# Adaptive-norm mixture-of-experts kernel: weights laid out by the host, condition matrices gathered block-diagonal

## The reference, cut to what matters

```python
w = weights[conditions]                              # (128, 32, 32), picked from a table of 200
h = einsum('bct,bcd->bdt', x, w)                     # mixes the 32 rows of a batch
scores = sigmoid(h @ gate_w.T)                       # 32 experts in 4 groups
# top 2 groups, then top 8 experts; cw = their normalised scores * 2.5, else 0
x_lat  = h @ fc1_w.T                                 # 256 -> 128
y_lat  = sum_e (relu(x_lat @ w1[e].T)**2 * cw[:, e]) @ w2[e].T
out = x + relu(h @ shared_up_w.T)**2 @ shared_down_w.T + y_lat @ fc2_w.T
```

## Time and profile before

| | us |
|---|---|
| median of 3 runs | 529.09 |
| lowest and highest | 527.57, 531.04 |
| span of the profiled execution, first to last instruction | 526.2 |
| TensorE busy in the span | 506.9 |
| DVE, ACT, POOL busy | 409.7, 371.0, 118.3 |

### The profile page before, as it was taken

The page is one execution under the profiler, slowest core; times in us unless marked ns, Lnnn a source line. Parts: engine busy times, 40 slices in busy tenths (PEclk is TensorE's granted clock), DMA queues, the critical chain, the costliest instruction groups (busy, mean ns, idle before and its releaser), DMA issues.

```text
span 526.2 us, 8694 instructions
## 1 busy us (share of the span) xinstructions
PE 506.9 (96%) x2558; PEld 430.6 (82%) x2558; DVE 409.7 (78%) x468; ACT 371.0 (71%) x495; POOL 118.3 (22%) x143
## 2 busy tenths in 40 slices
PE   4899999999999999999999989999999999999995
PEld 4788999788888888888888879978888888888874
DVE  1237954889899898988874696599899898988985
ACT  2247775788887878878754647478887878878780
POOL 4000000124243332423200000024243332423310
PEclk9899999999999999999999999999999999999998
DMA  6990007955555555555222001745555655555614
GB/s 164 283 236 1 2 6 198 344 209 191 186 188 197 199 197 189 182 197 190 81 70 90 2 0 22 241 154 192 192 182 197 199 193 199 178 197 189 200 41 161
DMA packets 42432, 83.37 MB, mean 158 GB/s; under 512 B 7168, under 2 KB 25520, under 8 KB 42416
## 3 DMA queue, kind: packets, MB, share of 16 engines
q1 hardware_dynamic: 42224, 82.62, 47.8%
q0 software_dynamic: 192, 0.54, 0.4%
HBM read 77.91 MB, written 5.24 MB: 158 GB/s over the span
## 4 chain that ended last, share of the span: by engine, by line
PE 90%; DVE 5%; DMA 2%; ACT 1%; issue 0%; SPq 0%; DVEq 0%
PE h_banks L553 33%; PE y_banks L566 33%; PE y_banks L514 8%; PE h_banks L488 6%; PE h_banks L440 2%; PE y_banks L464 2%; PE y_banks L470 2%; PE y_banks L418 1%; DMA scale_ring<-in_cond_w,cond_sb 1%; DVE act_lo L851 1%; PE y_banks L601 1%; DVE x_res L874 1%; DMA act_full<-in_gate_w 1%; PE y_banks L382 0%; DVE scale_ring L954 0%; DVE act_lo L866 0%
## 5 line engine op out<-in xcount | busy, mean ns | idle before, releaser
L358 POOL TENSOR_TENSOR w_ring<-experts_w,w_ring 128x128 fp32r<-128x128 f32 x128 | 112.5, 900 | 386.4 <-ACT w_ring L736 386.4
L851 DVE TENSOR_TENSOR act_lo<-act_full,act_hi 128x1024 fp32r<-128x1024 f32 x144 | 182.6, 1269 | 12.3 <-ACT act_full L711 9.9
L716 ACT ACTIVATE act_hi<-scaled 128x1024 fp32r<-128x1024 f32 x128 | 136.0, 1063 | 73.8 <-PE y_banks L566 43.4
L844 DVE SCALAR_TENSOR_TENSOR scaled<-h_banks,scale_ring 128x1024 f32<-128x1024 f32 x128 | 156.7, 1224 | 36.8 <-PE h_banks L553 31.4
L553 PE MATMUL h_banks<-lat_hi,w_ring 128*128 128x512 f32 x512 | 157.8, 389 | 0.0
L566 PE MATMUL y_banks<-act_hi,w_ring 128*128 128x512 f32 x512 | 137.3, 390 | 0.0
L719 ACT ACTIVATE act_full<-scaled 128x1024 f32<-128x1024 f32 x128 | 133.6, 1044 | 0.0
L566 PEld LDWEIGHTS y_banks<-act_hi,w_ring 128*128 128x128 f32 x512 | 95.8, 188 | 20.5 <-DVE x_res L860 0.7
L553 PEld LDWEIGHTS h_banks<-lat_hi,w_ring 128*128 128x128 f32 x512 | 95.9, 188 | 19.8
L553 PE MATMUL h_banks<-lat_lo,w_ring 128*128 128x512 f32 x256 | 99.6, 389 | 0.0
L566 PE MATMUL y_banks<-act_lo,w_ring 128*128 128x512 f32 x256 | 79.4, 391 | 0.9 <-DVE act_lo L851 0.9
(11 more groups left out here) (111 smaller groups left out, 424.5 us busy)
## 6 DMA issues: line engine op xcount, KB each, us to landing
scale_ring<-s_dram SPq DMA_DIRECT2D x128, 512.0 KB, 3.8
x_in<-in_x SPq DMA_DIRECT2D x8, 512.0 KB, 5.2
experts_w<-in_w SPq DMA_DIRECT2D x8, 512.0 KB, 7.9
out_x<-x_res SPq DMA_DIRECT2D x4, 512.0 KB, 2.9
out_x<-x_res SPq DMA_DIRECT2D x8, 256.0 KB, 3.2
scaled<-in_up_w SPq DMA_DIRECT2D x1, 512.0 KB, 4.1
scaled<-in_down_w SPq DMA_DIRECT2D x1, 512.0 KB, 5.1
cond_dram<-scale_ring SPq DMA_DIRECT2D x2, 256.0 KB, 4.9
```

Source lines behind the costliest of these rows:

```text
L358: pool.tensor_tensor(ring[:, slot, 1, :], experts_w[:, w, bass.ds(e, 1), :].rearrange("q a i -> q (a i)"), ring[:, slot, 0, :].bitcast(f32 ...
L716: act.activation(act_hi[:, half, :], scaled[:, half, :], ACT.Square).then_inc(act_hi_ready, 1)
L844: dve.scalar_tensor_tensor(scaled[:, half, :], h_banks[:, half, :], 0.0, scale_ring[:, scale_slot, :], ALU.max, ALU.mult).then_inc(scaled_ ...
L851: dve.tensor_tensor(act_lo[:, slot, :], act_full[:, slot, :], act_hi[:, slot, :].bitcast(f32), ALU.subtract).then_inc(act_lo_ready, 1)
```

## The change

1. The host hands over the weights transposed and laid out by partition: `up_w`, `down_w`, one tensor `rest_w` with fc1, fc2 and the zero-padded gate weight (768 columns), and `w1`, `w2` with their last two axes exchanged. All weight transposes on TensorE are gone: the 22 of the start and the 64 of the shared stage, with ACT's 16 copies and their waits. ACT and DVE split the small weights straight from SBUF; `rest_w` at the start, `up_w` and `down_w` behind block 1 of the projection.
2. The host builds a table of 4 x 200 x 32 rows of 128 floats, each condition matrix at each of the four diagonal places with zeros beside it. DVE works out row numbers from two loaded tensors of indices, and POOL gathers each tile of `cond_bd` with an indirect DMA of 128 rows of 512 bytes: 16 in pass 0, 16 for pass 1 behind them. The store to DRAM, the four loads of each pass and the zeroing are gone. POOL issues the bias behind the first four gathers, and the `affine_select` on `before` behind all 16 of pass 0. DVE's two waits ahead of its first `rest_of_projection` stay as they were.
3. `keep_warm` is one run of 24 transposes at the start. SP's order is: the two index tensors, x of block 0, `rest_w`, x of block 1, `up_w`, `down_w`, x of blocks 2 and 3, expert weights.

```diff
-SMALL_SPLITS = 4
+SMALL_SPLITS = 3
-WARM_UP = 12
+WARM_UP = 24
@@ SP
-            store_cond(0)
-            sp.dma_start(raw_fc1, fc1_w).then_inc(small_loaded, DMA)
-            sp.dma_start(raw_fc2, ...).then_inc(small_loaded, DMA)
-            sp.dma_start(raw_gate, gate_w).then_inc(small_loaded, DMA)
             load_x(0, 0)
-            sp.wait_ge(cond_zeroed, 1)
-            sp.wait_ge(cond_stored[0], DMA)
-            load_cond(0)
-            for b in range(1, BLOCKS):
+            sp.dma_start(raw_rest, rest_w).then_inc(rest_loaded, DMA)
+            load_x(0, 1)
+            sp.dma_start(raw_up, up_w).then_inc(up_loaded, DMA)
+            sp.dma_start(raw_down, down_w).then_inc(down_loaded, DMA)
+            for b in range(2, BLOCKS):
                 load_x(0, b)
-            for p in range(1, PASSES):
-                store_cond(p)
...
-                    sp.wait_ge(cond_stored[p + 1], DMA)
-                    sp.wait_ge(xc_ready, (p + 1) * BLOCKS)
-                    load_cond(p + 1)
@@ POOL
-            for p in range(PASSES):
-                pool.wait_ge(cond_idx_loaded[p], DMA)
-                pool.indirect_dma_start(
-                    cond_rows[:, p, :], None, cond_w.rearrange("s c d -> s (c d)"),
-                    bass.IndirectOffsetOnAxis(ap=cond_sb[:, p:p + 1], axis=0)).then_inc(cond_gathered[p], DMA)
+            def gather_cond(p, b):
+                if p > 0:
+                    pool.wait_ge(xc_ready, (p - 1) * BLOCKS + b + 1)
+                for n in range(BT * b, BT * (b + 1)):
+                    pool.indirect_dma_start(
+                        cond_bd[:, n, :], None, cond_w,
+                        bass.IndirectOffsetOnAxis(ap=cond_idx[:, p * TILES + n:p * TILES + n + 1], axis=0))\
+                        .then_inc(cond_gathered[b], DMA)
+            pool.wait_ge(cond_idx_ready, 1)
+            gather_cond(0, 0)
             pool.dma_start(bias_sb[:, :], ...).then_inc(bias_loaded, DMA)
+            for b in range(1, BLOCKS):
+                gather_cond(0, b)
             pool.affine_select(out=before[:, :, :], ...).then_inc(consts_ready, 1)
-            pool.memset(cond_bd[:, :, :], 0.0).then_inc(cond_zeroed, 1)
-            pool.memset(small_hi[:, GATE0:SMALL].bitcast(f32), 0.0).then_inc(gate_zeroed, 1)
-            pool.memset(small_lo[:, GATE0:SMALL].bitcast(f32), 0.0).then_inc(gate_zeroed, 1)
+            for p in range(1, PASSES):
+                for b in range(BLOCKS):
+                    gather_cond(p, b)
@@ PE
             pe.wait_ge(consts_ready, 1)
-            transpose_chunk(...)
             keep_warm(WARM_UP)
...
                 pe.wait_ge(x_loaded[b], (p + 1) * DMA)
-                pe.wait_ge(cond_loaded, (p + 1) * (BATCH_TILE * DMA))
+                pe.wait_ge(cond_gathered[b], (p + 1) * (BT * DMA))
...
-                    pe.wait_ge(wt_hi, SMALL_SPLITS)
-                    pe.wait_ge(wt_lo, SMALL_SPLITS)
+                    pe.wait_ge(wt_hi, 1)
+                    pe.wait_ge(wt_lo, 1)
...
             def shared_up(p, u):
+                if p == 0 and u == 0:
+                    pe.wait_ge(wt_hi, SMALL_SPLITS)
+                    pe.wait_ge(wt_lo, SMALL_SPLITS)
...
-                transpose_pair(p, 0)
-                transpose_pair(p, 1)
...
@@ ACT
-            round_chunk(0, small_hi[:, UP0:DOWN0], h_banks[:, 0, :])
...
+            round_small(rest_loaded, small_hi[:, FC1_0:SMALL], raw_rest)
...
+                    if p == 0 and b == 1:
+                        round_small(up_loaded, small_hi[:, UP0:DOWN0], raw_up)
+                        round_small(down_loaded, small_hi[:, DOWN0:FC1_0], raw_down)
...
-                copy_pair(p, 0)
...
@@ DVE
+            dve.wait_ge(cond_loaded, DMA)
+            dve.wait_ge(cond_row_loaded, DMA)
+            dve.scalar_tensor_tensor(cond_idx[:, :], cond_sb[:, :], float(C), cond_row_sb[:, :],
+                                     ALU.mult, ALU.add).then_inc(cond_idx_ready, 1)
+            rest_of_small(0, small_lo[:, FC1_0:SMALL], raw_rest, small_hi[:, FC1_0:SMALL])
...
-                    for stored in cond_stored:
-                        dve.wait_ge(stored, DMA)
...
                     for b in range(BLOCKS):
                         rest_of_projection(p, b)
+                        if b == 1:
+                            rest_of_small(1, small_lo[:, UP0:DOWN0], raw_up, small_hi[:, UP0:DOWN0])
+                            rest_of_small(2, small_lo[:, DOWN0:FC1_0], raw_down, small_hi[:, DOWN0:FC1_0])
```

More of the change, by code:

```diff
@@ L79, with adaln_ffn @@
 SMALL = GATE0 + HALVES * P
-def adaln_ffn(nc, x, cond, cond_w, gate_w, gate_b, fc1_w, fc2_w, w1, w2, up_w, down_w, out):
+def adaln_ffn(nc, x, cond, cond_row, cond_w, gate_b, up_w, down_w, rest_w, w1, w2, out):
     f32, f32r, i32 = mybir.dt.float32, mybir.dt.float32r, mybir.dt.int32
@@ L245, in _ @@
         def _(sp):
-            for p in range(PASSES):
-                sp.dma_start(cond_sb[:, p:p + 1], cond[p * PASS_BATCHES:(p + 1) * PASS_BATCHES]
-                             .rearrange("(b a) -> b a", a=1)).then_inc(cond_idx_loaded[p], DMA)
-            sp.dma_start(raw_up, up_w.rearrange("(k p) h -> p k h", p=P)).then_inc(up_loaded, DMA)
-            sp.dma_start(raw_down, down_w.rearrange("(a p) m -> p a m", p=P)).then_inc(down_loaded, DMA)
+            sp.dma_start(cond_sb[:, :], cond).then_inc(cond_loaded, DMA)
+            sp.dma_start(cond_row_sb[:, :], cond_row).then_inc(cond_row_loaded, DMA)
             def load_x(p, b):
@@ L373, in _ @@
         def _(pe):
-            def transpose_chunk(jobs):
-                for dst, src, n in jobs:
-                    last = pe.transpose(dst, src, ident[0:n, 0:n])
-                last.then_inc(wt_ready, 1)
             def keep_warm(n):
@@ L657, in _, with round_small @@
         def _(act):
[L658 to L659 removed]
+            def round_small(loaded, dst, src):
+                act.wait_ge(loaded, DMA)
                 act.activation(dst, src, ACT.Copy).then_inc(wt_hi, 1)
@@ L780, in _ @@
                     relu_shared(p, u + 1)
-                    copy_pair(p, 2 * u - 1)
                     if u == SHARED_UNITS - 3:
-                        act.wait_ge(experts_copied, 2 * W_CHUNKS)
-                        if p > 0:
+                        if p == 0:
+                            for loaded in raw_loaded:
+                                act.wait_ge(loaded, 2 * DMA)
+                        else:
                             act.wait_ge(experts_done, p * EXPERT_UNITS)
@@ L1050, with by_partition @@
     from concourse.bass_utils import run_bass_kernel_spmd
-    given = {"x": x, "cond": itok_B_1_198, "cond_w": L0_cond_weights, "gate_w": L0_ffn_gate_w,
-             "gate_b": L0_ffn_gate_bias, "fc1_w": L0_ffn_fc1_w, "fc2_w": L0_ffn_fc2_w, "w1": L0_ffn_w1,
-             "w2": L0_ffn_w2, "up_w": L0_ffn_shared_up_w, "down_w": L0_ffn_shared_down_w}
+    def by_partition(w, n):
+        return np.asarray(w).T.reshape(n, P, -1).transpose(1, 0, 2).reshape(P, -1)
+    cond_w = np.asarray(L0_cond_weights)
+    cond_table = np.zeros((BATCH_TILE, cond_w.shape[0], C, P), np.float32)
+    for j in range(BATCH_TILE):
+        cond_table[j, :, :, C * j:C * (j + 1)] = cond_w
+    cond = np.asarray(itok_B_1_198).astype(np.int32).reshape(B // BATCH_TILE, BATCH_TILE)
+    j, c = np.arange(P) // C, np.arange(P) % C
+    cond_row = np.broadcast_to((j * (cond_w.shape[0] * C) + c)[:, None], (P, B // BATCH_TILE)).astype(np.int32)
+    gate = np.zeros((P, H), np.float32)
+    gate[0:EXPERTS] = np.asarray(L0_ffn_gate_w)
+    rest_w = np.concatenate([by_partition(L0_ffn_fc1_w, HALVES), by_partition(L0_ffn_fc2_w, 1),
+                             by_partition(gate, HALVES)], axis=1)
+    given = {"x": x, "cond": np.repeat(cond.T, C, axis=0), "cond_row": cond_row,
+             "cond_w": cond_table.reshape(-1, P), "gate_b": L0_ffn_gate_bias,
+             "up_w": by_partition(L0_ffn_shared_up_w, HALVES),
+             "down_w": by_partition(L0_ffn_shared_down_w, SHARED_CHUNKS), "rest_w": rest_w,
+             "w1": np.asarray(L0_ffn_w1).transpose(0, 2, 1), "w2": np.asarray(L0_ffn_w2).transpose(0, 2, 1)}
     nc = bacc.Bacc("TRN2", target_bir_lowering=False, num_devices=1)
```

114 lines of the change are left out of this document (13 added, 101 removed).

## The result

The changed kernel takes 534.19 us (median of 5 runs, 532.67 to 535.73) against 529.09 us for the kernel before in the same comparison (5 runs, 527.57 to 531.04): ratio 1.0098, 95% interval 1.0067 to 1.0129. It is 5.1 us slower than the kernel before, and 6.1 us above the forecast of 528.1. The range of 522 to 534 just misses it.

The account below looks back on a forecast made before the run. TensorE was taken as the bound, with POOL's queue setting the new start. Later start 2.1, half clock 1.8 and shared stage -4.9 summed to -1.0 us: 528.1 us against 529.09, range 522 to 534.

Parts of the forecast that it names:

- POOL's queue sets the start: Start of pass 0: DVE's first xc_lo waits behind POOL's 16 gathers and bias DMA; project(0,2) starts 2.1 us later.
- 4.3 + 16 x 1.14 + 0.87 = 23.4 for consts_ready: POOL at the start: gathers begin at 4.3 us, take 1.14 each, then bias DMA 0.60 and select 0.27.
- The first rival: Flat price, POOL's gathers: 128 rows cost what 64 did, 0.99 us without gap; 525.7 us, chance 0.22.
- `project(0,2)` at half clock, +1.8 us: TensorE's third projection: after standing still for 4.2 us it runs at half clock, 1.8 us more.
- The landing doesn't decide: Last gathers of pass 0: landed by 26.1 us, at most 27.8, needed only at 31.3; landing takes some 3 us.
- The shared stage, -4.92: Shared stage of pass 0 without expert transposes: 55.81 us becomes pass 1's 50.89, DVE's routing taking back 2.2 of 7.1.
- a sign of being wrong: Wrong if ACT releases xc_lo, gathers cost under 0.9 or over 1.5 us, or the shared stage exceeds 52 us.
- The 16 gathers of pass 1 run on POOL from 23.5 to 42 ... so they have 36 us of cover: POOL behind pass 0's gathers: its next work before was at 78.14 us, so pass 1's gathers come at no cost.
- The sum, -1.0 us: Whole kernel: 2.1 later start plus 1.8 half clock minus 4.9 shared stage; span 526.2 to 525.2 us.
- Nothing from the shared stage: Rival, shared stage of pass 0: DVE hands over routing late, the 4.9 us are not got; 533.0 us, chance 0.10.

Follow-up runs that it names:

- SP's met wait: Changed kernel plus a wait on SP ahead of the expert loads, on a count already met since 3 us: 529.69 us, ratio 0.9989.
- the empty line: Changed kernel with one empty source line ahead of the gathers of pass 1, no instruction more or less: 530.64 us, ratio 1.0003.
- set A: Runs on one chip with the kernel before: select first 526.33, expert weights alone 525.19, old condition path 523.73, gathers of pass 1 later 529.24 us.
- the placebos: Changed kernel plus an already met wait on POOL (530.5 us), an empty source line (530.64 us), or an already met wait on SP (529.69 us).
- the later gathers: Changed kernel with the 16 gathers of pass 1 held until the scores are there: 529.24 us, ratio 1.0004.
- the held loads: Changed kernel with SP's eight expert-weight loads held until the fourth projection of pass 0 is done: 530.22 us, ratio 0.9986.
- set D: Runs on one chip with the kernel before: expert loads held 530.22, select first 525.89, that with 40 transposes 527.68, gathers later with 40 transposes 528.71 us.
- the 40 transposes: Changed kernel, gathers of pass 1 held until the scores, plus 40 transposes between project(0,1) and project(0,2): 528.71 us; with select first instead of held gathers: 527.68 us.
- set E: Runs on one chip with the kernel before: changed kernel with a met wait on POOL 530.5, an empty line 530.64, a met wait on SP 529.69 us.
- set B: Runs on one chip, including the changed kernel again 535.47, its gathers of pass 1 behind all projections 535.94, select first with gathers later 526.09 us.
- the version with the expert weights alone: Kernel before with only w1 and w2 transposed by the host, so the 64 expert transposes go: 525.19 us, ratio 0.9911.

## Why the prediction was right and wrong

| | before | forecast | changed, first profile | with SP's met wait | with the empty line |
|---|---|---|---|---|---|
| `project(0,2)` starts | 22.75 | 24.9 | 25.91 | 25.86 | 26.64 |
| shared stage starts | 37.49 | 41.4 | 48.10 | 42.02 | 44.19 |
| its length | 55.81 | 50.9 | 51.18 | 50.91 | 52.39 |
| span | 526.2 | 525.2 | 530.9 | 526.0 | 529.6 |

- *POOL's queue sets the start*: right. DVE's `xc_lo` follows the select. Putting the select first takes 3.8 us away in the profile of set A; by the ratios, 0.9937 and 0.9914 against the placebos' 0.9989 to 1.0003, it is worth 3 to 5 us. Within one set it is 2.9 us (526.33 for the later gathers' 529.24, set A) and 4.3 us (525.89 for the held loads' 530.22, set D).
- *4.3 + 16 x 1.14 + 0.87 = 23.4 for consts_ready*: 24.45. The gathers start sooner (3.70), but the period is 1.25 us, not 1.14: it was a mean over one gather with a gap and one without. That makes the start 1.0 us later than forecast. The busy time did not double with the rows: 128 rows of 512 bytes take 0.95 us where 64 of 4 KB took 1.08 and 0.90; that the length of a row has no part in it is not shown. So far the busy time agrees with the rule of the Trainium skill, "DMA: Bandwidth & Descriptors", section on the anatomy of one DMA on the GpSimd path, that many descriptors can be emitted before the incremental cost shows. The first rival's 0.99 us, too, was near the busy time. It is the 0.30 us gap, 4.8 us over 16 gathers, that this rival lost by: the gap stands there though POOL waits for nothing.
- *`project(0,2)` at half clock, +1.8 us*: right: 3.75 for 2.02, and the 40 transposes of set D show its cause, the stand-still ahead of it.
- *The landing doesn't decide*: right in this order, though its size was off: the first group leaves POOL at 8.55 and TensorE starts at 13.28, 4.7 us for my 3. With the select first, the landing is next to decide.
- *The shared stage, -4.92*: 50.91 in the best profile, and 4.7 us by the medians of the version with that edit alone. Not foreseen: that the wait for `act_lo`, which I took from pass 1 as 2.1 us, in other executions costs 1.5 us of clock as well. There the stage lasts 52.4 us, over the 52 that the prediction named as a sign of being wrong.
- *"The 16 gathers of pass 1 run on POOL from 23.5 to 42 ... so they have 36 us of cover"*: this is the step that failed in the measured comparison. POOL was free, as it said. But beside the gathers of both passes TensorE's signals and its stream were held up: 4.8 us in `project(0,3)` and 0.9 in the stages around it. The prediction put the cost of these gathers to TensorE at nothing. No part of the sum had a term for it, and neither had a rival. Without these 5.7 us the time would have come out near 528.5, so this step, and not the period of a gather (1.0 us), is what made the forecast fail. Why the gathers hold up TensorE there stays open. On the three chips of sets A, D and E the step holds: with the gathers of pass 1 held back (ratio 1.0004) and in place (1.0003 and 0.9994) the times are the same.
- *The sum, -1.0 us*: on the chip of set E the version with the empty line comes to +0.3 us (530.64 for 530.31), with an interval from -1.3 to +1.6. By the profile with the full clock in the shared stage, +4.5 at the start and -4.9 in the stage, the span is 0.2 us shorter. There the forecast of -1.0 stands, as it lies within that interval. In the first comparison and in set B it is wrong by 6 to 7 us.
- *Rivals*: none of them came in. Nothing from the shared stage gave the nearest number (533.0) for a reason that the profile denies.

What stays open is what differs between the chips. The profiles exclude the clock (in the hole of the first profile it is granted in full until 37 us), a semaphore (the transposes ask for none), POOL's standing wait, and the program (the empty line). The expert loads had ended by about 30 us, the hole comes at 32.6 to 37, and the transposes still advance in steps at 36 to 38; holding the loads was not tried on a chip that shows the hold-up, and neither were the placebos; nor did the changed kernel's own file run in sets A, D and E. So that it is the chip, and not the hour or something else that was constant within a set, is inferred from the division of the sets. Every execution here is recorded by the profiler, and just the held-up ones lack records of landings and of who released whom. Either what holds up the signals also loses records, or the recording itself takes part; only an execution without the recording could tell, and there is none. A version in which twelve of the sixteen gathers of pass 1 have a tile of their own, and so wait for nothing of TensorE, has no result.

## What to carry to other kernels

Before work is put into a queue, look for every count that stands behind it there: one `affine_select` of 0.24 us behind 16 gathers cost 3.8 us, and one moved line gives them back. A gain found by one part alone (the expert weights laid out by the host, 4.7 us) should be kept apart from a part that loses. And compare edits only with the unedited kernel in the same set on the same chip: each of five edits seemed to cure the hold-up, and so did an empty line; the kernel before, present in every set, could not warn, since what varies between the sets touches only the kernels with the gathers. When records that should be there are missing from a profile, as the landings were here, note it before the edits are read: this sign on the page divided the two kinds of sets without an exception.

## What the runs showed of the hardware that was not expected

- Back-to-back indirect DMAs on POOL keep a period of 1.25 us, 0.95 busy and 0.30 gap, with 128 rows each. In most profiles one to six of the 32 take longer, 1.3 to 2.0 us, and then all behind them is late.
- In some sets, and so it seems on some chips, TensorE's signals reach ACT and POOL 4 to 9 us late beside such gathers and up to 3.5 us behind the last of them, and its stream advances in steps of 0.7 us or a multiple of it, even where it waits for nothing. In others the same instructions show nothing of it. The profiles of the first kind lack most records of the gathers' landings.
- A wait of 2.1 us in a busy TensorE is followed, in some executions, by 24 products of which most run at half clock (4.59 us, granted clock 0.50 in 60 to 63 us of the version with the expert weights alone), in others not (3.11 us, granted clock 1.00 all through, with SP's met wait).
